# Recurrent mixer on one core: pair products in two banks instead of four, one ring of six banks, two mixes moved to VectorE, levels placed by predicated copies

## What is computed

```python
# x is the layer-normed input
delta = shifted - x                       # shifted: the token before
z   = tanh((x + delta * mu_x) @ W_x1.T)   # five groups of 32
mus = einsum(z, W_x2) + x_bias            # five mixes: r, w, k, v, g
r = (x + delta * r_mu) @ W_r.T            # and so k, v, g; w by way of a tanh of rank 64
w = -exp(w)
# four heads, 32 keys x 64 values, scanned over the tokens of a sequence:
o_t = q_t (S + u * k_t v_t);  S = exp(w_t) * S + k_t v_t
# then a norm per head, gn_weight, gn_bias, * silu(g), @ W_o.T, + the layer's input
```

## Time and profile before

| | us |
|---|---|
| median of 3 runs | 3771.62 (3766.94 to 3772.66) |
| the profiled execution's own time | 3765.53 |
| its span, first to last instruction | 3763.7 |
| the mixer's first load to its last store (L843) | 0.7 to 991.0 |

### The profile page before, as it was taken

The page is one execution under the profiler, slowest core; times in us unless marked ns, Lnnn a source line. Parts: engine busy times, 40 slices in busy tenths (PEclk is TensorE's granted clock), DMA queues, the critical chain, the costliest instruction groups (busy, mean ns, idle before and its releaser), DMA issues. The chain is left out here.

```text
span 3763.7 us, 76874 instructions
## 1 busy us (share of the span) xinstructions
PE 3349.6 (89%) x30948; PEld 1936.6 (51%) x30948; DVE 2525.1 (67%) x4722; ACT 2001.1 (53%) x2927; POOL 824.6 (22%) x919
## 2 busy tenths in 40 slices
PE   7888888888589984999999999999999999977998
PEld 3454545445367762444444444444444444436777
DVE  4656566565477762786777867778687776816776
ACT  2333433333155540476666766667666666664554
POOL 3444444444212221010201011020110201011222
PEclk8887878788599995799999999999999999998999
DMA  1000000000111114121221212212122222111110
GB/s 47 13 13 24 21 15 24 13 18 11 60 59 52 51 48 72 34 40 22 64 39 46 41 27 58 41 44 41 34 51 41 47 38 40 33 47 48 46 51 34
DMA packets 110466, 145.67 MB, mean 39 GB/s; under 512 B 21632, under 2 KB 94352, under 8 KB 109328
## 3 DMA queue, kind: packets, MB, share of 16 engines
q1 hardware_dynamic: 109344, 137.93, 15.6%
q0 software_dynamic: 768, 2.82, 0.4%
HBM read 53.97 MB, written 38.41 MB: 25 GB/s over the span
## 5 line engine op out<-in xcount | busy, mean ns | idle before, releaser
L1753 DVE TENSOR_REDUCE b_half_max<-banks 128x1 f32<-128x512 f32 x2048 | 1315.3, 686 | 444.6 <-PE banks L1478 262.5
L1704 ACT ACTIVATE b_p_t<-banks 128x1024 f32<-128x1024 f32 x1024 | 1047.0, 1025 | 397.2 <-PE banks L1478 255.9
L1534 PE MATMUL banks<-b_k_stack,b_q_stack 62*128 62x512 f32 x2048 | 829.3, 478 | 34.2 <-issue 17.8
L1595 PE MATMUL banks<-b_q_stack,b_k_stack 64*128 64x512 f32 x2048 | 851.7, 469 | 0.0
L1550 PE MATMUL banks<-b_p_t,b_v 128*17 128x256 f32 x8192 | 640.9, 385 | 25.1 <-ACT b_pv L1673 24.5
L1595 PEld LDWEIGHTS banks<-b_q_stack,b_k_stack 64*128 64x128 f32 x2048 | 342.9, 185 | 432.2 <-issue 416.7
L1478 PE MATMUL banks<-b_tables,b_halves 64*128 64x128 bf16 x4096 | 437.3, 224 | 0.0
L1534 PEld LDWEIGHTS banks<-b_k_stack,b_q_stack 62*128 62x128 f32 x2048 | 337.8, 188 | 68.4 <-issue 26.0
L1094 ACT ACTIVATE ffn_relu<-banks,ffn_scale_fc 128x512 f32<-128x512 f32 x256 | 176.3, 688 | 272.9 <-PE banks L1030 272.9
L1043 PE MATMUL banks<-ffn_proj_t,ffn_r_hi 128*128 128x256 f32 x1024 | 257.1, 285 | 2.5 <-DVE ffn_r_lo L1213 2.5
L1550 PEld LDWEIGHTS banks<-b_p_t,b_v 128*17 128x17 f32 x8192 | 135.9, 95 | 225.3 <-issue 75.7
(11 more groups left out here) (230 smaller groups left out, 4893.1 us busy)
## 6 DMA issues: line engine op xcount, KB each, us to landing
ffn_x<-x SPq DMA_DIRECT2D x32, 512.0 KB, 3.9
b_q_stack<-b_qk_hi SPq DMA_DIRECT2D x256, 64.0 KB
b_k_stack<-b_qk_hi SPq DMA_DIRECT2D x256, 64.0 KB
a_x<-hidden_states SPq DMA_DIRECT2D x16, 512.0 KB, 3.9
x<-a_x SPq DMA_DIRECT2D x16, 512.0 KB, 2.9
x<-ffn_x SPq DMA_DIRECT2D x16, 512.0 KB, 2.9
b_x<-x SPq DMA_DIRECT2D x8, 1024.0 KB, 5.4
b_k_stack<-b_qk_lo SPq DMA_DIRECT2D x128, 64.0 KB
```

The source lines that it names most:

```text
L1534: last = pe.matmul(m, q_stack[rows, slot, qb * P:(qb + 1) * P], k_stack[rows, slot, half * BANK:(half + 1) * BANK], start=True, stop=not h ...
L1595: last = pe.matmul(out, k_stack[stack, slot, kb * P:(kb + 1) * P], q_stack[stack, slot, half * BANK:(half + 1) * BANK], start=True, stop=n ...
L1704: act.activation(p_t[use % P_BUFS][:, :, :], scores[use % 2], ACT.Exp, scale=slopes()[pair][0]).then_inc(p_made, 1)
L1753: dve.tensor_reduce(half_max[:, (pair + rg * PAIRS) * QB + qb, half:half + 1], misc.at["max", g, turn], axis=AX.X, op=ALU.max, negate=True ...
```

## The change

- `products` now takes two banks (6 and 7), two heads in each: per head 256 columns, of which levels 0 to 5 take 224 and the far product 32. The far product is made in two halves of 32 later tokens, one in partitions 0 to 63, one in 64 to 127, so by eight matmuls instead of four.
- Because two heads share a bank, PE makes the products of heads 0 and 2 first, then those of heads 1 and 3; between them come the transpose of k and a wait for the first half (`half_multiplied`).
- The banks 0 to 5 form one ring for everything else.
- The adds of mixes 0 and 1 move from POOL to DVE, behind the fourth scaling; POOL keeps three, three places later in its order. `mix_made` becomes `first_mixes` and `last_mixes`.
- Level 0 is masked as before (now 128 x 256 elements). Levels 1 to 5 are no longer masked and summed: five `copy_predicated` take them from the banks and put them at their places, where an int32 mask (`mask_bits`, made once) says so.
- ACT's far copies (now two) and PE's next pair products wait for `levels_added` (all five).

```diff
-        products = banks[:, 4:8, :]
+        products = banks[:, 6:8, :].rearrange("p b (h n) -> p (b h) n", h=HEADS_A // 2)
...
-        front = Ring([banks[:, 0, :], banks[:, 1, :]], (zeroed, 1))
-        back = Ring([banks[:, 2, :], banks[:, 3, :]], (zeroed, 1))
+        ring = Ring([banks[:, i, :] for i in range(6)], (zeroed, 1))
...
+        def mixed(c, j):
+            return (first_mixes, 2 * c + j + 1) if j < 2 else (last_mixes, 3 * c + j - 1)
...
                     if t:
-                        pe.wait_ge(halves_added, t)
+                        pe.wait_ge(levels_added, LEVELS_ADDED * t)
                         pe.wait_ge(far_placed, t)
-                    for l in range(NEARBY):
-                        kk, qq = ks[l], qs[l]
+                    for heads in ((0, 2), (1, 3)):
+                        for l in range(NEARBY):
+                            for at in range(0, P, BLOCK):
+                                now = slice(tok + at, tok + at + BLOCK)
+                                for h in heads:
+                                    r = slice(h * HK, (h + 1) * HK)
+                                    out, moving = products[at:at + BLOCK, h, LEVEL[l]:LEVEL[l + 1]], qs[l][r, now]
+                                    if l:
+                                        out, moving = out.rearrange("p (n m) -> p n m", m=1 << l), upper(moving, l)
+                                    pe.matmul(out, ks[l][r, now], moving, start=True, stop=True, tile_position=(h * HK, at))
                         for at in range(0, P, BLOCK):
+                            late = tok + BLOCK + at // 2
+                            for h in heads:
                                 r = slice(h * HK, (h + 1) * HK)
+                                last = pe.matmul(products[at:at + BLOCK, h, LEVEL[NEARBY]:], ks[NEARBY][r, tok:tok + BLOCK],
+                                                 qs[NEARBY][r, late:late + BLOCK // 2], start=True, stop=True, tile_position=(h * HK, at))
+                        if heads[0] == 0:
+
+                            last.then_inc(half_multiplied, 1)
+                            b, (used, n) = ring.take(("k", c, i), (k_tok_made, t + 1))
+                            pe.wait_ge(used, n)
+                            pe.transpose(b[:, 0:P], ks[TREE][:, tok:tok + P], ident[:, :]).then_inc(k_turned, 1)
+                            pe.wait_ge(half_multiplied, t + 1)
                     last.then_inc(multiplied, 1)
...
-                    act.wait_ge(halves_added, t + 1)
+                    act.wait_ge(levels_added, LEVELS_ADDED * (t + 1))
...
+                    for at in range(0, P, BLOCK):
+                        late = BLOCK + at // 2
+                        last = act.activation(weights[0:BLOCK, :, late:late + BLOCK // 2], products[at:at + BLOCK, :, LEVEL[NEARBY]:], ACT.Copy)
+                    last.then_inc(far_placed, 1)
...
+                    if i == 3:
+                        for own in range(2):
+                            dve.wait_ge(mu_scaled, 10 * c + SCALED[own])
+                            dve.tensor_tensor(mix(own)[:, :, :], mix(own)[:, :, :], xt[:, :, 1:], ALU.add).then_inc(first_mixes, 1)
...
-                    dve.tensor_tensor(near[:, :, :], products[:, :, 0:MASKED],
-                                      mask[:, 0:MASKED].unsqueeze(1).to_broadcast([P, HEADS_A, MASKED]), ALU.mult).then_inc(masked_made, 1)
+                    dve.tensor_tensor(near[:, :, :], products[:, :, 0:BLOCK],
+                                      mask[:, 0:BLOCK].unsqueeze(1).to_broadcast([P, HEADS_A, BLOCK]), ALU.mult).then_inc(masked_made, 1)
                     dve.wait_ge(masked_made, t + 1)
-                    dve.scalar_tensor_tensor(out=upper(sums, NEARBY - 1), in0=level(products, NEARBY - 1), scalar=mask[:, MASKED:MASKED + 1],
-                                             in1=upper(sums, NEARBY - 1), op0=ALU.mult, op1=ALU.add).then_inc(halves_added, 1)
-                    dve.wait_ge(halves_added, t + 1)
-                    for l in range(1, NEARBY - 1):
+                    for l in range(1, NEARBY):
+                        picked = level(mask_bits, l).unsqueeze(1).to_broadcast([P, HEADS_A, BLOCK >> (l + 1), 1 << l])
+                        moved = products[:, :, LEVEL[l]:LEVEL[l + 1]].rearrange("p h (n m) -> p h n m", m=1 << l)
                         if l > 1:
                             dve.wait_ge(levels_added, LEVELS_ADDED * t + l - 1)
-                        dve.tensor_tensor(upper(sums, l), upper(sums, l), level(near, l), ALU.add).then_inc(levels_added, 1)
+                        dve.copy_predicated(upper(near[:, :, :], l), picked, moved).then_inc(levels_added, 1)
...
             def prepare(c):
                 xt, levels = xn_t[c % 2], carry(c)
-                yield
-                for j in range(MIXES):
+                for _ in range(3):
+                    yield
+                for j in range(2, MIXES):
                     pool.wait_ge(mu_scaled, 10 * c + SCALED[j])
-                    pool.tensor_tensor(mix(j)[:, :, :], mix(j)[:, :, :], xt[:, :, 1:], ALU.add).then_inc(mix_made, 1)
+                    pool.tensor_tensor(mix(j)[:, :, :], mix(j)[:, :, :], xt[:, :, 1:], ALU.add).then_inc(last_mixes, 1)
```

More of the change, by code:

```diff
@@ L63, in constants @@
     parts = [(s == t) | (s // 2 == t // 2) & (s % 2 == 0) & (t % 2 == 1)]
-    for level in range(1, NEARBY - 1):
+    for level in range(1, NEARBY):
         m = 1 << level
         parts.append(((s // (2 * m) == t // (2 * m)) & (s // m % 2 == 0))[:, t[0] // m % 2 == 1])
-    parts.append(s < BLOCK // 2)
     c["c_mask"] = np.concatenate(parts, 1).astype(np.float32)
@@ L254, in normalize @@
                 for kt in range(KT):
-                    b, (used, n) = front.take(("xt", c, kt), (xt_made, 2 * c + kt + 1))
+                    b, (used, n) = ring.take(("xt", c, kt), (xt_made, 2 * c + kt + 1))
                     pe.wait_ge(used, n)
@@ L266, in normalize @@
                 for m in range(2):
-                    b, (used, n) = front.take(("z", c, m), (z_made, 2 * c + m + 1))
+                    b, (used, n) = ring.take(("z", c, m), (z_made, 2 * c + m + 1))
                     pe.wait_ge(used, n)
@@ L285, in mix_in @@
                         rows = slice(rows.start, rows.start + LOWRANK)
-                        b, (used, value) = front.take(("mu", c, j, kt), (mu_scaled, 10 * c + i + 1))
+                        b, (used, value) = ring.take(("mu", c, j, kt), (mu_scaled, 10 * c + i + 1))
                         pe.wait_ge(used, value)
@@ L291, in project @@
                 def project(w, j, name, used_up, ready, rows=P):
-                    b, (used, n) = front.take((name, c), used_up)
+                    b, (used, n) = ring.take((name, c), used_up)
                     pe.wait_ge(used, n)
-                    pe.wait_ge(mix_made, MIXES * c + j + 1)
+                    pe.wait_ge(*mixed(c, j))
                     pe.matmul(b[0:rows, :], w[:, 0, :], mix(j)[:, 0, :], start=True, stop=False)
@@ L299, in token_major @@
                     for h in range(2):
-                        b, (used, n) = front.take((name, c, h), (used_by, 2 * c + h + 1))
+                        b, (used, n) = ring.take((name, c, h), (used_by, 2 * c + h + 1))
                         pe.wait_ge(used, n)
-                        pe.wait_ge(mix_made, MIXES * c + j + 1)
+                        pe.wait_ge(*mixed(c, j))
                         for i in range(2):
@@ L317, in prepare @@
                 yield
-                b, (used, n) = front.take(("w", c), (decay_made, 2 * c + 1))
+                b, (used, n) = ring.take(("w", c), (decay_made, 2 * c + 1))
                 pe.wait_ge(used, n)
@@ L373, in advance @@
                     keys, weights = k_tok[t % 2], pair[t % 2]
-                    b, (used, n) = back.take(("kv", c, i), (state_made, t + 1))
+                    b, (used, n) = ring.take(("kv", c, i), (state_made, t + 1))
                     pe.wait_ge(used, n)
@@ L381, in advance @@
                     last.then_inc(kv_ready, 1)
-                    b, (used, n) = back.take(("o", c, i), (o_made, t + 1))
+                    b, (used, n) = ring.take(("o", c, i), (o_made, t + 1))
                     pe.wait_ge(used, n)
@@ L408, in finish @@
                 for kt in range(KT):
-                    b, (used, n) = back.take(("o_t", c, kt), (o_t_made, 2 * c + kt + 1))
+                    b, (used, n) = ring.take(("o_t", c, kt), (o_t_made, 2 * c + kt + 1))
                     pe.wait_ge(used, n)
@@ L416, in finish @@
                 for i in range(CT):
-                    b, (used, n) = back.take(("y", c, i), (y_added, 4 * c + i + 1))
+                    b, (used, n) = ring.take(("y", c, i), (y_added, 4 * c + i + 1))
                     pe.wait_ge(used, n)
@@ L451, in normalize @@
                     rows = Z_ROWS[m]
-                    act.activation(z[0:rows, m, :], front.at["z", c, m][0:rows, :], ACT.Tanh).then_inc(z_made, 1)
```

(10 more changed lines are left out.)

72 lines of the change are left out of this document (30 added, 42 removed).

## The result

| | us |
|---|---|
| changed kernel, median of 4 runs | 3638.85 (3638.03 to 3639.64) |
| kernel before, beside it, median of 4 runs | 3770.89 |
| ratio | 0.9651 (95%: 0.9634 to 0.9668) |
| span of the profiled execution | 3636.2, from 3763.7 |

In the span it is 127.5 us. The first turn of outputs comes at 119.75 us instead of 135.63 (15.9 us); the twelve periods behind it take 51.27 us each instead of 60.00 (734.98 - 119.75 and 855.65 - 135.63, by 12), which is 104.8 us; the last steps give the remaining 7. The mixer's last store is issued at about 866 us; the forecast had 916.

A forecast was written before the change was run, and what follows sets the result against it. DVE's queue was taken to bound the mixer's first stretch and PE the second; -3.5 and -2.1 made -5.6 us a period, times 14 = -78, with the tail -75: 3771.6 to 3696 us, range 3650 to 3748.

The forecast's parts named there:

- Stalls, ring: PE's stalls before v and the third output product go with one ring of six: 3.5 us, second stretch.
- Pair products: On PE, 13.7 ns a record and a break between halves: +0.7 us per pair, bounds +0.25 and +1.4.
- Copies and multiply: On DVE, a pair's mask work takes 2.40 us instead of 2.57: -0.34 us for the first stretch's two pairs.
- Waits that move: PE's pair products wait for all levels and two ACT copies: nothing in full periods, about +3 us once at the end.
- First stretch: From `mix_in(0)` to the output turn, DVE's queue falls from 20.49 to 20.2 us; mean -3.5 us a period.
- The credit of the collision to the moved mixes: In DVE's first stretch, POOL's later adds no longer block the second pair's sums: -1.67 us, against +2.44 for the adds.
- Second stretch: From output turn to next `mix_in(0)`, PE-bound: two stalls gone, -3.5, two dearer pairs, +1.4: -2.1 us a period.
- rival 1: PE's clock also rises in the second stretch, another 4.5 us a period: 3633 us; chance 0.10.
- Number of periods: The mixer's gain of 5.6 us a period was multiplied by 14: -78 us, with the tail -75.
- Rival 2: Pairs at +1.4 us and copies at 0.53 us leave 2.1 us a period: 3745 us; chance 0.15.
- Rival 3: PE's clock stays down and rises late in the second stretch, 3.9 us a period slower: 3826 us; chance 0.08.
- Rival 4: A slow user (gate, y) holds a ring bank, one stall returns: 3.9 us a period, some 3720; chance 0.05.

The follow-up runs named there:

- b_shared: The kernel before with one edit, its own four spare banks as one shared ring instead of two rings of two: 3641.6 us, ratio 0.9653.
- four_ring: The changed kernel with products in four banks again, without halves, and one shared ring of four; DVE mixes and predicated copies kept: 3649.38 us, ratio 0.9682.
- shared_copies: b_shared with the levels placed by predicated copies, mixes left on POOL: 3622.68 us, ratio 0.9607.
- b_halves: The kernel before with pair products in two halves of two heads, k's transpose and a wait between them, still four banks: 3809.52 us, ratio 1.0101.
- sums: The changed kernel with the levels masked and summed as before instead of placed by predicated copies: 3662.7 us, ratio 0.9711.
- pool_mixes: The changed kernel with the first two mix adds back on POOL at their old places: 3643.91 us, ratio 0.9660.
- b_dve_mixes: The kernel before with the first two mix adds on DVE, nothing else: 3742.82 us, ratio 0.9929.
- busy_waits: The changed kernel with four discarded matmuls before the first half of v and four before the third output product: 3691.5 us, ratio 0.9789.
- old_waits: The changed kernel with the two old PE stalls put back as waits, before v and before the third output product: 3714.31 us, ratio 0.9852.
- fill: The changed kernel with four discarded matmuls before PE's wait at tile 1's pair products: 3646.69 us, ratio 0.9676.
- late_fill2: The changed kernel with POOL's last three adds held until `a_o` is scaled, discarded matmuls before tile 1's pair products and tile 0's state product: 3642.64 us, ratio 0.9658.

## Why the prediction was wrong in size

- **Stalls, ring.** Right: both stalls went, 3.5 us a period. And more than that was right: the sharing is the change. What I had not seen is that four banks are enough for it (b_shared), so that the price of two-bank products, +0.7 us a pair, bought little: 10.5 us net beside four_ring, and shared_copies, without that price and without the moved mixes, is 16 us faster than the changed kernel.
- **Pair products.** Right: 13.3 ns a record, 2.15 us a pair, +37 us in b_halves. The two terms of the 0.7 (0.3 and 0.4 forecast, 0.4 and 0.3 measured) were each a little off.
- **Copies and multiply.** 2.2 us a pair instead of 2.40, within the bounds; worth 24 us in sums, of which I had 14 x 0.34 = 5 in the sum. 7 us of it come before the first turn.
- **Waits that move.** Costed at nothing. PE's wait at the pair products of tile 1 is 1.5 us a period (18.5 us in twelve), all in the first stretch, and filling it gained 0.2 us in most periods.
- **First stretch.** Forecast -3.5 us, measured (26.12 + 24.37) / 2 - (21.02 + 21.66) / 2 = -3.9; over all twelve periods it is 25.5 - 21.3, -4.3. Right in mechanism and near in size; that DVE's queue was forecast to 0.1 us is in part luck, as the terms above show. The credit of the collision to the moved mixes was wrong: in pool_mixes, and in b_shared with sums and POOL's adds as before, it leaves the pairs too and shows up at xn.
- **Second stretch: the step that failed.** "Second stretch: -3.5 + 1.4 = -2.1" leaves the clock's penalty where it was. Without it the stretch before would be 30.0 + 3.5 - 1.4 = 32.1 us; b_dve_mixes has such stretches, 32.14 us at a clock of 1.00. Measured were 37.43 and 33.79, so the penalty was 5.3 and 1.7 us, not "9.0 and 0": the error of the window. The changed kernel has none. Over the two periods shown the stretch fell by 5.6 us a period instead of 2.1; over all twelve it fell from 34.5 to 30.0, by 4.5, of which 2.4 is the clock. And busy_waits against old_waits shows the link: idling at these places takes the clock down, work of the same length does not. It was rival 1, with 0.10; its argument against, that the clock falls in the first stretch, is true (0.68, 0.61) but costs little there, since DVE sets the end (halving it in fill gained 0.2 us in most periods). Its 3633 us stand near the 3638.85 partly by luck: it had 4.5 us a period for the clock, from the wrong window, and nothing for the start.
- **Number of periods.** I counted 14 and nothing before them. The two preparing steps and the first stretch behind them alone gained 15.9 us, 11 of them by the ring (b_shared's first turn comes at 124.54). PE's waits for a bank of the front ring are in them too (8.9 us of waits of L288 before 135 us).
- **The sum again:** 12 x 8.73 + 15.9 + 7 = 127.5 us. Of the 52 us of span that were missed, 16 are the start, 10 the end (7 gained where I had 3 lost), and 12 x 3.1 = 38 the periods, 28 of them the clock in the second stretch and 9 the first; against them stand 11 us for two periods that I had counted too many.
- **Rival 2** fell: neither the pairs nor the copies came near their far ends. **Rival 3**, slower by the clock, fell: the stretch behind the turn rose to full clock. **Rival 4** fell: no bank is held by a slow user.

What stays open: how much of the 31 us that the moved mixes gain in the kernel before, and of the 18 that they lose on the shared ring, is DVE's queue and how much the clock. The start of w_a moves by 0.7 us earlier and 0.6 later, which gives the sign; no run separates the two sizes. Letting ACT copy the far products while DVE still reads the same banks was not tried.

## What to carry to other kernels

Two small rings for two families of results make each wait for its own slowest user; one ring in the order of use lets the long holders of one family stand behind the short ones of the other, at no cost in banks. Try that single edit before paying for more buffers: here it was the whole gain. Of the other parts only the copies paid on top of it (19 us), and the fastest kernel measured has the shared ring of four and the copies alone. When a stretch is bound by PE, count a stall at more than its length (75 us against 53 here), and check the ends of the windows against the repeating instruction on both sides before building a sum on them.

## What the runs showed of the hardware

- The clock of PE can fall where PE hardly idles: in late_fill2 PE is busy in 33.08 of 33.08 us at 0.90, every second period, while the same stretch between them runs at 1.00. Taking away half clock at one place (14.8 to 3.7 us a period) brought it back at a dearer one.
- A DVE instruction with one SBUF tensor and scalars per partition can be blocked by POOL as well: the scaling of xn took up to 2.09 us instead of 0.41 in pool_mixes, while POOL's add of a mix ran (471.94 to 473.95 us, beside the row shown).
- A predicated copy of 128 x 128 elements with an int32 mask, from a bank, takes 0.30 us (0.291 to 0.446), no more than an add of the same size between SBUF tensors (0.29).
- Matmuls on four tiles of 32 rows by 64 columns start 13.3 ns apart at full clock and on eight tiles 10 ns: halving the tiles in use cost a third, not double. At half clock the spacings are some 24 ns (40 records in 1.27 us at 464.18) and 13.7 ns: with four tiles it nearly doubles with the clock, with eight it does not.
